# A graph layer and expert kernel on one core: what stands where, and which load comes how, at the changes between its stages

## The chip, the cores and the metric

The kernel runs on one core of a Trainium2 chip. The metric is the device time of one execution in microseconds (us). TensorE (PE in the profile) multiplies, VectorE (DVE) and ScalarE (ACT) work on elements, GpSimd (POOL) and SyncE (SP) mostly start transfers. ACT starts some transfers too; each of these engines works its own instruction list in order.

## The reference: what is computed

```
x = layernorm(x)                                    # 10000 nodes, 512 channels
for l in 0, 1, 2:
    agg = segment_sum(x[src], dst) / max(deg, 1)    # 20000 edges, sorted by dst
    out = agg @ Wl + bl + x @ Wr
    x = where(out >= 0, out, a * out)
x = x0 + x                                          # x0: the input
xn = layernorm(x)
cw = top 2 of softmax(xn @ Wr + br), 8 experts
x = x + sum over e of cw[e] * (relu(xn @ W1[e] + b1[e]) @ W2[e] + b2[e])
```

## The kernel before, in words

Nodes are worked in 79 tiles of 128 rows, edges in 157 tiles of 128. All node rows stay in SBUF in one tensor, `res`. Two buffers serve tiles in turn (slot 0 for even tiles, slot 1 for odd ones), and nearly every semaphore is kept for each slot. Since (agg / deg) @ Wl equals the sum over edges of rows of x @ Wl, each layer has two stages.

**Dense stage** (`dense`, and `first_dense` for layer 0). PE turns a tile of x (`x_transpose`, into psT), ACT and DVE apply the slopes to it in its turned form (`keep_xT` on ACT; `bend` on DVE), and PE makes y = x @ Wl. ACT copies y out (`take_y`), SP stores it to DRAM (`store_y`, y_rows). In layers 1 and 2 a product of full precision is made from three products at a higher rate: `y_high` (w_high, x_high), `y_low` (w_low, x_low) and `y_cross` (w_cross, x_cross). DVE makes x_high, x_low and x_cross for each tile (`high_x`, `split_x`) and, once a layer, the parts of the weights: `split_high` (w_cross and w_part, from the raw weights in wy), `split_cross` (w_high and w_cross) and `split_low` (w_low, which is written over wz, so it waits for the last z product). `next_x` on DVE makes the x of a tile: the gathered sum times 1/deg plus the tile's z.

**Sum stage.** POOL gathers rows of y from DRAM by `src` (`gather_edge`, eight buffers), ACT and DVE split them in two parts (`high`, `low`), PE sums them within an edge tile by a product with a selection matrix (`segment_sum`, L710 and L711), ACT copies the sums out and stores them in DRAM (sum_rows). Between the segment sums PE makes z = x @ Wr (`z_product`, `z_half`), and DVE adds the bias to it and puts it back in `res` (`take_z`). Nine z tiles, the late ones, are kept for the end of the stage. There the sums of segments that run over several edge tiles are mended: PE multiplies the starting rows (L747), DVE adds the result to gathered rows (L1385), POOL scatters them to sum_rows, and only then gathers sums by node (`gather_node`). On DVE the order of all this is written out by hand, between the nine late `take_z`.

**Expert stage.** For each tile two streams are woven together on DVE (`experts`): the part `ahead` makes x, its residual sum with the input rows (loaded by SP into `outs`, `load_x`) and its moments, and ends in POOL's and ACT's `norm`; the part `own` takes the router's logits, finds the top two experts, and adds the bias b1 (in bvec) to the hidden layer. PE's order is in `x_turn`, `router`, `hidden_turn`, `up` and `down`.

Three places where one stage meets the next are touched. wz holds Wr for the z products, but in the dense stage of layers 1 and 2 it holds w_low; so ACT starts Wr's load (`load_z`, L874) only once the last `y_low` is done, and then bl's load, and then copies the last two y tiles out. The raw Wl for the next layer comes from SP near the end of the sum stage. At the end of layer 2 SP loads W1, a, b2, the rows of x for tiles 0 and 1, and then, when all z tiles are taken, b1 (into bvec), W2 (into wz) and the rows of x for tiles 2 and 3.

## Time and profile before

| | us |
|---|---|
| median of 3 runs | 2687.99 |
| lowest and highest | 2687.64, 2690.53 |
| the profiled execution | 2686.95 |
| its span | 2685.2 |
| TensorE busy in it | 2625.3 (98%) |
| VectorE, ScalarE, GpSimd busy | 1805.6, 1272.2, 990.5 |
| mean granted TensorE clock | 0.994 of full speed |

The span runs from the first to the last instruction of the profiled execution; 1.75 us of its time lie outside. TensorE's span holds all stages one after the other, so time is lost where it stands idle or runs at its lower clock. The stages lie about so: dense 0 to 350 us, sums of layer 0 to 676, dense of layer 1 from 702 to 955, its sums to 1315, dense of layer 2 from 1319 to 1575, its sums to 1937, experts to the end.

### The profile page before, as it was taken

What the parts mean: (1) busy time and instruction counts of PE and PEld (TensorE: products, weight loads), DVE (VectorE), ACT (ScalarE), POOL (GpSimd) and SP (SyncE); (2) the same over time, 40 slices, a digit from 0 to 9 for tenths busy, and PEclk for the clock granted to TensorE, in tenths of its full rate; (3) what the DMA queues carried; (4) which work ended last, traced back from release to release, by engine and by line L of the source; (5) the groups of instructions that cost most, each with busy time, mean ns of one, the idle gap of its engine ahead of it and who ended that gap; (6) DMA issues with size and microseconds to landing.
All of it is one profiled execution on the core that took longest, in us unless ns stands there. A gap on an engine that the chain in (4) does not pass through costs nothing.

```text
span 2685.2 us, 39728 instructions
## 1 busy us (share of the span) xinstructions
PE 2625.3 (98%) x9195; PEld 1506.2 (56%) x9195; DVE 1805.6 (67%) x5090; ACT 1272.2 (47%) x2681; POOL 990.5 (37%) x1054
## 2 busy tenths in 40 slices
PE   7999999999999999999999999999899999999999
PEld 3444445554688855555588855555455555555554
DVE  5555555554899955555699955555477777777775
ACT  2222245554588855555388855555122222222222
POOL 2222255553344445554233335555122222222221
PEclk9999999999999999999999999999999999999999
DMA  4444378887355568887355558888422222222221
GB/s 133 133 133 133 118 224 270 266 271 229 100 164 164 164 214 263 274 263 257 97 164 165 164 181 273 263 274 263 145 78 82 82 86 90 82 82 85 87 85 48
DMA packets 200943, 446.57 MB, mean 166 GB/s; under 512 B 34383, under 2 KB 34695, under 8 KB 200836
## 3 DMA queue, kind: packets, MB, share of 16 engines
q0 software_dynamic: 64928, 207.55, 27.2%
q10 hardware_dynamic: 69168, 126.12, 12.9%
q1 hardware_dynamic: 66740, 111.54, 11.9%
q8 instruction: 59, 0.97, 0.1%
q14 instruction: 48, 0.39, 0.0%
HBM read 238.50 MB, written 207.11 MB: 166 GB/s over the span
## 4 chain that ended last, share of the span: by engine, by line
PE 94%; DMA 2%; DVE 2%; ACT 1%; issue 1%; SPq 0%; POOL 0%; DVEq 0%; POOLq 0%; ACTq 0%
PE psY L590 11%; PE psH L570 10%; PE psY L570 10%; PE psM L698 9%; PE psY L698 9%; PE psH L698 8%; PE psT L564 6%; PE psY L604 5%; PE psY L612 5%; PE psY L621 5%; PE psS L710 4%; PE psS L711 4%; PE psM L570 2%; PE psH L590 1%; PE psS L564 1%; PE psH L799 1%
## 5 line engine op out<-in xcount | busy, mean ns | idle before, releaser
L498 POOL DMA_INDIRECT rows<-y_rows,lists x471 | 485.4, 1031 | 475.7 <-PE psS L711 355.0
L1175 DVE TENSOR_TENSOR lows<-rows,highs 128x512 fp32r<-128x512 f32 x471 | 326.2, 693 | 374.1 <-ACT highs L832 366.6
L505 POOL DMA_INDIRECT rows<-sum_rows,nodeI x237 | 296.0, 1249 | 329.7 <-DVE rows L1183 295.7
L832 ACT ACTIVATE outs<-psS 128x512 f32<-128x512 f32 x471 | 279.8, 594 | 284.5 <-PE psS L711 284.0
L832 ACT ACTIVATE highs<-rows 128x512 fp32r<-128x512 f32 x471 | 294.8, 626 | 143.5 <-ACT outs L832 109.7
L710 PE MATMUL psS<-highs,sel 128*128 128x512 f32 x471 | 348.7, 740 | 7.2 <-ACT outs L832 7.2
L479 POOL TENSOR_TENSOR st<-st,small 128x1 f32<-128x1 f32 x158 | 89.9, 569 | 664.1 <-DVE st L1075 664.1
L590 PE MATMUL psY<-wy,res 128*128 128x512 f32 x632 | 286.6, 596 | 0.7 <-ACT res L832 0.7
L570 PE MATMUL psY<-wy,xTs 128*128 128x512 f32 x632 | 285.2, 594 | 0.0
L570 PE MATMUL psH<-wz,hTs 128*128 128x512 f32 x632 | 284.2, 592 | 0.7 <-ACT hTs L832 0.7
L698 PE MATMUL psM<-wz,res 128*128 128x512 f32 x544 | 255.5, 592 | 0.0
L698 PE MATMUL psY<-wz,res 128*128 128x512 f32 x536 | 251.7, 592 | 0.0
L698 PE MATMUL psH<-wz,res 128*128 128x512 f32 x528 | 248.0, 592 | 0.0
L832 ACT ACTIVATE outs<-psY 128x512 f32<-128x512 f32 x237 | 141.8, 598 | 221.3 <-PE psY L590 213.8
L946 ACT ACTIVATE rows<-res,st 128x512 f32 (+1 forms) x79 | 64.2, 813 | 361.4 <-POOL st L547 361.4
L564 PE MATMUL psT<-ident,rows 128*128 128x128 f32 x1264 | 197.5, 279 | 23.0 <-ACT rows L946 8.0
L570 PEld LDWEIGHTS psH<-wz,hTs 128*128 128x128 f32 x632 | 120.0, 190 | 151.7 <-issue 150.7
L843 ACT ACTIVATE res<-psS,acol 128x128 f32 (+1 forms) x632 | 180.7, 369 | 20.8
L604 PE MATMUL psY<-w_high,x_high 128*128 128x512 f32 x632 | 186.6, 417 | 0.0
L711 PE MATMUL psS<-lows,sel 128*128 128x512 f32 x471 | 186.2, 395 | 0.0
L564 PEld LDWEIGHTS psT<-ident,rows 128*128 128x128 f32 x1264 | 145.6, 141 | 67.3 <-issue 45.5
L590 PEld LDWEIGHTS psY<-wy,res 128*128 128x128 f32 x632 | 114.7, 192 | 115.6 <-issue 114.5
(166 smaller groups left out, 4109.7 us busy)
## 6 DMA issues: line engine op xcount, KB each, us to landing
sum_rows<-outs ACTq DMA_DIRECT2D x471, 256.0 KB, 3.7
y_rows<-outs SPq DMA_DIRECT2D x237, 256.0 KB, 2.0
rows<-in_x POOLq DMA_DIRECT2D x78, 256.0 KB, 2.9
outs<-in_x SPq DMA_DIRECT2D x78, 256.0 KB, 2.6
out_rows<-res SPq DMA_DIRECT2D x78, 256.0 KB, 2.0
rows<-y_rows,lists POOLq DMA_INDIRECT x471, 4.2
rows<-sum_rows,nodeI POOLq DMA_INDIRECT x237, 3.5
wy<-in_L_gnn_Wl SPq DMA_DIRECT2D x3, 1024.0 KB, 7.3
```

The source lines that it names most:

```text
L498: pool.indirect_dma_start(out=rows[:, t % RING, :], out_offset=None, in_=y_d, in_offset=bass.IndirectOffsetOnAxis(ap=col(srcT, t), axis=0) ...
L505: pool.indirect_dma_start(out=rows[:, s, :], out_offset=None, in_=s_d, in_offset=bass.IndirectOffsetOnAxis(ap=col(nodeI, t), axis=0), boun ...
L564: mm = pe.transpose(dest[:, c * P:(c + 1) * P], tile[:, c * P:(c + 1) * P], ident[:, :])
L570: mm = pe.matmul(dest, xT[:, c, :], w[:, c, :], start=(c == 0), stop=(last and c == C - 1))
L590: mm = pe.matmul(dest, part(t, c), w[:, c, :], start=(c == 0), stop=(c == C - 1))
L604: mm = pe.matmul(psY[s][:, :], x_high[:, q * P:(q + 1) * P], w_high[:, q, :], start=(q == 0), stop=False, skip_group_check=True)
L698: mm = pe.matmul(psZ(l, s), part(t, q), wz[:, q, :], start=(q == 0), stop=(q == C - 1))
L710: pe.matmul(psS[g % 2][:, :], sel[:, g, :], highs[:, g, :], start=True, stop=False)
L711: pe.matmul(psS[g % 2][:, :], sel[:, g, :], lows[:, t % RING, :], start=False, stop=True)\
L832: act.activation(o, i_, ACT.Copy).then_inc(signal, 1)
L843: x_ = act.activation(part(t, q), psS[s][:, q * P:(q + 1) * P], ACT.Copy, scale=acol[:, k - 1, q:q + 1])
L1175: dve.tensor_tensor(lows[:, t % RING, :], rows[:, t % RING, :], highs[:, g, :].bitcast(F32), ALU.subtract)\
```

## The change

Six edits.

1. The late end of the sum stage, on DVE: the second late `take_z` and the mended rows' additions stand ahead of `split_high`, which waits for the raw weights.
2. Also there: the third tile's x (`next_x(0, 2)`) and the second tile's `bend` stand ahead of `split_low`, and not after the last `take_z`, in the first `split_x`.
3. On PE the third tile's turn stands first in `dense`. In layer 1 the first `y_high` writes the PSUM tile that the last z product filled, so it now waits by name for the last `take_z` there.
4. Wr of layers 1 and 2 is loaded in four parts of 128 rows, each with a semaphore, and the first z product waits for each part ahead of the multiplication that reads it.
5. SP loads the rows of x for tiles 2 and 3 ahead of its wait for all z tiles, so ahead of b1 and W2.
6. DVE waits for b1 ahead of the first addition of it, and not ahead of the whole first `experts`.

```diff
@@ SP
                     for c in range(2):
                         load_x(sp, 0, c, outs, var_in, 1, xe_in)
+                    for c in (2, 3):
+                        load_x(sp, 0, c, outs, var_in, 1, xe_in)
                 all_turns(sp, z_sb, l + 1)
...
-            for c in (2, 3):
-                load_x(sp, 0, c, outs, var_in, 1, xe_in)
@@ PE
             def dense(k):
                 pe.wait_ge(high_parts, k)
+                x_transpose(0, 2, k)
+                if k == 1:
+                    pe.wait_ge(z_sb[0], uses(0))
...
-                    if not (isinstance(i, int) and 2 * i + c + 2 >= NT):
+                    if not (first or isinstance(i, int) and 2 * i + c + 2 >= NT):
                         x_transpose(i, c + 2, k)
...
+            def first_z(l):
+                pe.wait_ge(z_sb[0], l * uses(0))
+                for q in range(C):
+                    pe.wait_ge(wz_row[q], 16 * l)
+                    mm = pe.matmul(psZ(l, 0), part(0, q), wz[:, q, :], start=(q == 0), stop=(q == C - 1))
+                mm.then_inc(z_ps[0], 1)
...
-                pe.wait_ge(wz_in, 16 * (l + 1))
-                z_product(0, 0, l)
+                if l == 0:
+                    pe.wait_ge(wz_in, 16)
+                    z_product(0, 0, l)
+                else:
+                    first_z(l)
...
-            pe.wait_ge(wz_in, 16 * (LAYERS + 1))
+            pe.wait_ge(wz_in, 32)
@@ ACT, load_z
-                act.dma_start(wz[:, :, :], Wr[l].rearrange("(c p) n -> p c n", p=P)).then_inc(wz_in, 16)
+                for q in range(C):
+                    act.dma_start(wz[:, q, :], Wr[l][q * P:(q + 1) * P, :]).then_inc(wz_row[q], 16)
@@ DVE, split_x
                 if not (isinstance(i, int) and i + c == 0):
                     high_x(i, c, k)
-                if not (isinstance(i, int) and 2 * i + c + 2 >= NT):
-                    next_x(i, c + 2, k)
-                if not (isinstance(i, int) and 2 * i + c + 1 >= NT):
-                    bend(i, c + 1, k)
+                    if not (isinstance(i, int) and 2 * i + c + 2 >= NT):
+                        next_x(i, c + 2, k)
+                    if not (isinstance(i, int) and 2 * i + c + 1 >= NT):
+                        bend(i, c + 1, k)
@@ DVE, experts
                     dve.wait_ge(hT_ps[s], n)
+                    if isinstance(i, int) and i + c == 0:
+                        dve.wait_ge(bvec_in, 16 * (LAYERS + 1))
                     k_h = step(dve.tensor_tensor(h, psY[s][:, :], bvec[:, :], ALU.add))
@@ DVE, the end of a layer
                 take_z(*late[0], l)
-                if l + 1 < LAYERS:
-                    split_high(l)
                 take_z(*late[1], l)
...
                        .then_inc(mend_add, 1)
+                if l + 1 < LAYERS:
+                    split_high(l)
                 take_z(*late[2], l)
...
                     take_z(*late[-2], l)
+                    next_x(0, 2, l + 1)
+                    bend(0, 1, l + 1)
                     split_low(l)
                     take_z(*late[-1], l)
...
-            dve.wait_ge(bvec_in, 16 * (LAYERS + 1))
             dve.wait_ge(small_in, 32)
```

On DVE, at the end of layer 0's sums, stood before (res<-psY is `take_z`, rows<-rows,psS the mended rows' additions, w_cross<-wy and w_part `split_high`):

```order
L1164 TENSOR_TENSOR res<-psY,bvec 128x512 x3
L1234 TENSOR_SCALAR w_cross<-wy 128x512 x4
L1235 TENSOR_TENSOR w_part<-wy,w_cross 128x512 x4
L1164 TENSOR_TENSOR res<-psY,bvec 128x512
L1385 TENSOR_TENSOR rows<-rows,psS 128x512
L1385 TENSOR_TENSOR rows<-rows,psS 29x512
L1164 TENSOR_TENSOR res<-psY,bvec 128x512
L1238 TENSOR_TENSOR w_high<-wy,w_part 128x512 x4
```

On DVE at the same place stands now:

```order
L1179 TENSOR_TENSOR res<-psY,bvec 128x512 x4
L1400 TENSOR_TENSOR rows<-rows,psS 128x512
L1400 TENSOR_TENSOR rows<-rows,psS 29x512
L1249 TENSOR_SCALAR w_cross<-wy 128x512 x4
L1250 TENSOR_TENSOR w_part<-wy,w_cross 128x512 x4
L1179 TENSOR_TENSOR res<-psY,bvec 128x512
L1253 TENSOR_TENSOR w_high<-wy,w_part 128x512 x4
```

One `take_z` and both additions moved from behind the eight instructions of `split_high` to ahead of them.

A little later on DVE, at the start of the dense stage of layer 1, stood before (rows<-rows,rdeg,res is `next_x`, res<-psT,res `bend`):

```order
L1164 TENSOR_TENSOR res<-psY,bvec 128x512
L1246 TENSOR_SCALAR w_low<-w_part 128x512 x4
L1164 TENSOR_TENSOR res<-psY,bvec 128x512
L1183 SCALAR_TENSOR_TENSOR rows<-rows,rdeg,res 128x512
L1190 SCALAR_TENSOR_TENSOR res<-psT,res 128x512
L1212 TENSOR_TENSOR x_low<-res,x_high 128x512
L1215 SCALAR_TENSOR_TENSOR x_cross<-x_low,res 128x512
```

On DVE there stands now:

```order
L1179 TENSOR_TENSOR res<-psY,bvec 128x512
L1198 SCALAR_TENSOR_TENSOR rows<-rows,rdeg,res 128x512
L1205 SCALAR_TENSOR_TENSOR res<-psT,res 128x512
L1261 TENSOR_SCALAR w_low<-w_part 128x512 x4
L1179 TENSOR_TENSOR res<-psY,bvec 128x512
L1227 TENSOR_TENSOR x_low<-res,x_high 128x512
L1230 SCALAR_TENSOR_TENSOR x_cross<-x_low,res 128x512
```

Between the last `take_z` and x_low no instruction is left; `next_x` and `bend` moved ahead of w_low.

On SP, at the end of layer 2's sums, stood before (wy<-in_L_ffn_W is W1, wz<-in_L_ffn_W is W2, bvec<-in_L_ffn_b is b1):

```order
L413 DMA wy<-in_L_ffn_W 128x4x64 x8
L367 DMA avec<-in_L_gnn_a 128x512
L417 DMA b2s<-b_rows 32x512
L358 DMA outs<-in_x 128x512 x2
L367 DMA bvec<-in_L_ffn_b 128x512
L364 DMA wz<-in_L_ffn_W 128x4x512
L358 DMA outs<-in_x 128x512 x3
```

On SP there stands now:

```order
L414 DMA wy<-in_L_ffn_W 128x4x64 x8
L368 DMA avec<-in_L_gnn_a 128x512
L418 DMA b2s<-b_rows 32x512
L359 DMA outs<-in_x 128x512 x4
L368 DMA bvec<-in_L_ffn_b 128x512
L365 DMA wz<-in_L_ffn_W 128x4x512
L359 DMA outs<-in_x 128x512
```

Two of the loads of x moved from behind W2 to ahead of b1.

## Rows read from the trace of the kernel before

**Rows 1.** Windows: a dense stage, a sum stage; us, busy of each engine, PEclk, DMA, GB/s

```profile
720.00:940.00 220.00, 220.00 (x1102) 181.65 (x1101) 206.45 (x344) 193.30 (x481) 102.06 (x69) 1.00 0.51 165
975.00:1276.00 301.00, 298.59 (x831) 156.07 (x830) 175.39 (x371) 174.87 (x306) 153.00 (x150) 1.00 0.83 266
```

**Rows 2.** Waits of PE, whole span: line, waited for, total us, times, longest

```profile
PE psT L564 <- issue: 6.4, 2, 3.2
```

**Rows 3.** Timeline, end of layer 0's sums: start us, us, what, idle before

```profile
671.55 1.43 DVE L1234 TENSOR_SCALAR w_cross<-wy 128x512 fp32r<-128x512 f32 x4 [6.25 <-DMA wy<-in_L_gnn_Wl]
...
676.15 1.26 DVE L1385 TENSOR_TENSOR rows<-rows,psS 128x512 f32<-128x512 f32 x2
...
683.86 7.13 PE L590 MATMUL psY<-wz,res 128*128 128x512 f32 x16 [0.44 <-DVE res L1164]
...
700.37 0.69 DVE L1164 TENSOR_TENSOR res<-psY,bvec 128x512 f32<-128x512 f32 x1 [0.15 <-DVE w_low L1246]
...
702.36 0.68 DVE L1212 TENSOR_TENSOR x_low<-res,x_high 128x512 fp32r<-128x512 f32 x1
```

**Rows 4.** Timeline: the mending products of layers 0 and 1, an addition in layer 2

```profile
667.84 3.04 PE L747 MATMUL psS<-rows,hTs 128*128 128x512 f32 x6
...
1286.21 3.04 PE L747 MATMUL psS<-rows,hTs 128*128 128x512 f32 x6
...
1909.93 0.68 DVE L1385 TENSOR_TENSOR rows<-rows,psS 29x512 f32<-29x512 f32 x1 [0.28 <-PE psS L747]
```

**Rows 5.** Chain that ended last, layer 1 to 2: start us, us, what

```profile
1288.31 1.44 DVE w_cross L1234 x4
...
1315.49 3.20 issue
...
1325.32 0.91 PE psY L621 x4
```

**Rows 6.** Windows: PE at the start of layer 2's dense stage, and of the experts

```profile
1318.70:1325.32 6.62, 6.62 (x21) 5.43 (x22) 4.86 (x8) 3.51 (x10) 2.72 (x2) 0.55 0.15 40
701.94:706.00 4.06, 3.66 (x19) 2.85 (x20) 4.03 (x7) 2.75 (x7) 1.74 (x2) 1.00 0.23 65
1950.90:1958.90 8.00, 7.99 (x26) 5.47 (x27) 4.60 (x23) 1.63 (x5) 0.83 (x3) 0.67 0.13 33
```

**Rows 7.** Timeline, from layer 1's dense stage into its sums

```profile
953.20 0.44 ACTq L874 DMA_DIRECT2D wz<-in_L_gnn_Wr  x1
...
959.06 5.40 PE L590 MATMUL psH<-wz,res 128*128 128x512 f32 x8 [3.98 <-DMA wz<-in_L_gnn_Wr]
963.12 1.01 POOL L498 DMA_INDIRECT rows<-y_rows,lists  x1 [22.79 <-DMA y_rows<-outs]
...
966.74 0.63 ACT L832 ACTIVATE highs<-rows 128x512 fp32r<-128x512 f32 x1 [11.03 <-DMA rows<-y_rows,lists]
```

**Rows 8.** Chain that ended last: first z half in layers 1 and 2

```profile
972.25 1.72 PE psM L698 x4
...
1592.84 1.72 PE psM L698 x4
```

**Rows 9.** Transfers by line: KB each, us from issue to landing

```profile
outs<-in_x SPq DMA_DIRECT2D x78, 256.0 KB, 2.6
```

**Rows 10.** Timeline, layer 2: the first z product, POOL's first gather

```profile
1578.65 6.39 PE L590 MATMUL psH<-wz,res 128*128 128x512 f32 x8 [3.97 <-DMA wz<-in_L_gnn_Wr]
1581.31 1.01 POOL L498 DMA_INDIRECT rows<-y_rows,lists  x1 [21.84 <-DMA y_rows<-outs]
```

**Rows 11.** Timeline, start of the experts: PE, DVE, DVE, PE

```profile
1937.88 1.03 PE L570 MATMUL psM<-wgs,xTs 128*128 128x8 f32 x8 [0.78 <-ACT xTs L832]
...
1941.74 0.17 DVE L1266 SCALAR_TENSOR_TENSOR sm<-psM,bgs 128x8 f32<-128x8 f32 x1 [4.34 <-DMA bvec<-in_L_ffn_b]
...
1945.30 0.69 DVE L1280 SCALAR_TENSOR_TENSOR outs<-rows,outs 128x512 f32<-128x512 f32 x1 [2.01 <-DMA outs<-in_x]
...
1950.91 1.09 PE L564 MATMUL psT<-ident,rows 128*128 128x128 f32 x4 [8.03 <-ACT rows L946]
```

More of the change, by code:

```diff
@@ L212, in build @@
         wz_in = sem("wz_in")
+        wz_row = sems("wz_row", C)
         bvec_in = sem("bvec_in")
```

## The prediction

> **What bounds the kernel now.** I read windows first. TensorE (PE) is busy for the whole of a dense stage's 220 us, and for 298.59 of 301 us of a sum stage, at full clock [rows 1]. So inside a stage PE sets the time, and time can only be won where one stage meets the next. The list of PE's waits, the timeline around each meeting, and the chain that ended last then give five places:
>
> - Layer 0 to 1, and 1 to 2: PE waits 3.2 us ahead of the third tile's turn, twice [rows 2]; "issue" there only means that no single record released it. The timeline does: DVE makes w_low, takes the last z, makes the third x, bends, and only then makes x_low, all after the last z product. Ahead of this DVE waits 6.25 us for the raw weights [rows 3], with mended rows and z tiles queued behind that wait.
> - Dense stage to sums, layers 1 and 2: PE waits 3.98 and 3.97 us for Wr, and its next product takes 5.40 and 6.39 us [rows 7, 10], where two products in a row take 7.13 [rows 3], so 3.5 each.
> - Sums to experts: PE waits 8.03 us for the normed third tile [rows 11]. Its work is late because DVE waits 4.34 us for b1, then 2.01 us for the input rows of that tile [rows 11], which were issued behind b1 and W2.
>
> The clock comes on top. After 3.2 us of waiting in layer 2's start the granted clock is 0.55 over 6.62 us, but 1.00 after the same wait in layer 1's, and 0.67 over 8.00 us in the experts' start [rows 6]. The two levels are 1.2 and 2.4 GHz, so 0.55 is nearly all at the lower one.
>
> **Edit 1, mended rows ahead of raw weights.** It takes 1.26 us of additions and one take_z (0.69) from between w_part and the product that waits for DVE, 1.95 us in all [rows 3]. In exchange split_high can start only after the additions: the mending product's start plus its 3.04 us plus an addition of 0.68 [rows 4]. Layer 0: 667.84 + 3.72 = 671.56, against 671.55 when the weights let w_cross start [rows 3]. Nothing is lost, and PE wins **1.9**: product three no longer waits and the later wait is met with DVE 1.9 us further. Layer 1: 1286.21 + 3.72 = 1289.93 against 1288.31 [rows 4, 5], 1.6 later, so **0.3** remains. The mended rows' scatter and the gathers by node start earlier too, but they are behind other work already. Bounds: 0 to 1.9 and -0.5 to 0.3.
>
> **Edits 2 and 3, the third tile.** In layer 1 the z tile's take ends at 700.37 + 0.69 = 701.06, and x_low starts at 702.36 [rows 3]. next_x and bend now stand in the time in which DVE waits for the last z product, so x_low follows the take at once: **1.3**. y_high waits for the same take by name (its PSUM tile), so PE idles as long at first, but it is no later for x_low than DVE.
> In layer 2 the tile is another one, and turn and y_high run at once behind the last z product, T = 1315.49. Before, the first y_cross stands at 1325.32, T + 9.83 [rows 5]. Now DVE is free for x_low at T + 2.3: in layer 1 the wait ended at 701.94 [rows 6] and was 3.2 long [rows 2], so T was 698.74 and the take's end T + 2.3. Four whole-tile instructions of about 0.65 (0.69 by itself, some of it overlapped) give the fourth tile's x at T + 4.9. The five pieces from 1318.70 to 1325.32 are 6.62 x 0.55 = 3.6 us of work at full clock [rows 6]; the last two, a turn (half a product) and a product, are 1.4 of it. So y_cross stands at T + 6.3: **3.5** won, of which 3.0 is the clock. PE's wait is now cut in two, about 1.6 and 1.0 us, and I take it that the clock stays up. If it falls, 1.4 is left. That is the range of the term.
>
> **Edit 4, Wr in quarters.** A 256 KB load of this kind lands in 2.6 us [rows 9]; the whole of Wr took 5.86 (953.20 to 959.06, rows 7). So the first part should land at 955.8 and the last near 959.1, as the bytes are the same. Each multiplication is 0.9 (7.13 / 8, rows 3), so the first z product ends at 960.0 where it ended at 964.46. Two more products end near 967.0. Now something else is late: the first edge. POOL gathers it at 963.12, ACT starts on it at 966.74 for 0.63 [rows 7], DVE needs another 0.69, which is 968.1. The second edge is a gather behind (1.01 and a bit), with half a microsecond of sums: the first z half starts at 969.8 where it was 972.25 [rows 8]: 2.4. Three more issues of 0.44 [rows 7] stand on ACT ahead of its last two copies of y, whose stores POOL's gathers wait for: 0 to 1.3 later. I take 0.8, for part of it is hidden by stores that queue behind the load anyway: **1.7** in layer 1. In layer 2, 1581.31 [rows 10] + 3.62 + 0.63 + 0.69 = 1586.25, with 1.7 again 1587.95, against 1592.84 [rows 8]: 4.9, less 0.8, **4.1**; PE is ready at 1578.65 + 0.94 + 7.0 = 1586.6. Bounds: -1.3 to 2.4 (the clock falls in the new wait of about 2 us; a fall costs up to 6.39 - 3.5 = 2.9, rows 10), and 0.9 to 4.9.
>
> Against this edit speaks the Trainium skill, "DMA: Bandwidth & Descriptors", Rules for kernel authors: for full bandwidth a transfer should have at least 1 MiB. Its Anatomy section fits a transfer, one issued from GpSimd, as about 2.0 us plus its bytes at 436 GB/s. By that fit, an estimate from the page, a quarter is 2.6 us, as the row shows, and four of them are 10.4 us if the fixed parts don't overlap; the sum would then lose nearly all of this edit. The row decides only for one quarter; how four in a queue overlap no row of this load shows.
>
> **Edits 5 and 6, start of the experts.** The logits are there at 1937.88 + 1.03 = 1938.9, and DVE now starts then, not at 1941.74: 2.84. The 2.01 us for the rows of x go too, for they are issued before b1 [rows 11]. PE's turn comes 4.85 earlier, at 1946.06; b1 landed at 1941.7 and its first use is past that. The wait that is left is 8.03 - 4.85 = 3.2 us, as long as the two after which the clock once fell and once didn't. The 8.00 us of work behind it are 8.00 x 0.67 = 5.4 at full clock [rows 6]. So 4.9 are won if the clock falls as before, 7.5 if not; I take the middle, **6.1**. The two loads cost SP nothing: both moments they wait for come before the last z tile.
>
> **Sum.** 1.9 + 1.3 + 0.3 + 3.5 + 1.7 + 4.1 + 6.1 = 18.9. The profiled execution took 2686.95, so 2668.05; the median is 1.04 above it: **2669**. All upper ends give 1.9 + 1.3 + 0.3 + 3.5 + 2.4 + 4.9 + 7.5 = 21.8, or 2666; all lower ends 0 + 1.3 - 0.5 + 1.4 - 1.3 + 0.9 + 4.9 = 6.7, or 2681.
>
> **Rivals.**
> - *Quarters don't overlap.* Each part takes the 2.6 us of a lone one [rows 9], 10.4 in all, so the first z product ends at 953.20 + 10.4 + 0.9 = 964.5, as before: nothing in layer 1, and 0.9 in layer 2, where that product took 1.0 longer. 18.9 - 5.8 + 0.9 = 14.0, 2674. For it: stores and bl's load share the engines. Against it: many transfers are in flight in every stage at 165 to 266 GB/s [rows 1].
> - *The sum stage gives the start back.* Were the gathers and not PE its bound (266 GB/s, a DMA share of 0.83, rows 1), the 5.8 of edit 4 would be gone at its end: 13.1, 2675. Against it: PE's 2.4 us idle in 301.
> - *The clock falls in the new waits* in layer 1's sums, at layer 2's dense start and in the experts: 18.9 - 3.0 - 2.1 - 1.2 = 12.6, 2675.
> - *Slower: the last y stores.* ACT's four issues hold back the copies on which all gathers wait. With a delay of d in both layers edit 4 gives 7.3 - 2 d, and the other edits 13.1, so it decides from d = 10.2 on; 5.4 slower, 2693, is d = 12.9. Against it: ACT's added issues are 1.3 us.
> - *The change does little.* Something not in the records, such as a later release of PE in the experts' start, keeps edits 5 and 6 from counting, and two of the above come with it: under 5 won, 2684.
>
> **Chances.** The forecast 0.70, by itself from 2665 to 2673; quarters 0.08; given back 0.07; clock 0.08; slower 0.02; little 0.05. A difference under 0.2% (5.4 us) can't be told from none here. Faster 0.93, same 0.05, slower 0.02. The range of 2664 to 2676 takes in the first three rivals and leaves out the last two and odd mixtures.
>
> **What would show it.** In the profile after: L1400's additions ahead of L1249, with PE's wait near 676 gone and one of under 1 us near 681; the 3.2 us waits of rows 2 gone or cut, and y_cross of layer 2 some 6.3 us behind the last z product at a granted clock of 1.00; PE's first z product starting less than 1 us after the dense stage, its four parts about 0.9 apart, and the new wait for an edge behind it; POOL's first gather at most 1.3 us later against the load's issue; in the experts no wait for b1 or x and a PE wait of about 3.2 us. The prediction is wrong if the quarters land together at the end, if POOL's first gather moves by more than 2 us, or if the experts' start keeps its 8 us.

## The result, and the profile after

| | before | after |
|---|---|---|
| median of 4 runs, us | 2689.23 | 2671.27 |
| lowest and highest | 2687.64, 2690.53 | 2669.96, 2673.41 |
| ratio of times, 95% interval | | 0.9934 [0.9917, 0.9951] |
| the profiled execution | 2686.95 | 2673.41 |
| its span, its granted clock | 2685.2, 0.994 | 2671.8, 0.997 |

The table of before ahead of the prediction had three of these four runs. The change saves 18.0 us by the medians. The two profiled executions differ by 13.5 only: that of before was faster than all four runs of its median, that of after is the slowest of its four. Of all executions behind this document one was disturbed (before_fill, 10552.56 us at a granted clock of 0.557), and it is left out. The four runs after took 2673.41, 2672.07, 2670.47 and 2669.96 us at a mean granted clock of 0.997, 0.997, 0.998 and 0.999. So the clock is part of the result, and a trace shows one draw of it.

Windows of the changed kernel: the same two steady stretches as in [rows 1], then PE behind its wait at the start of layer 1's dense stage, of layer 2's, and of the experts. The columns are those of [rows 1], PEclk third from the end.

```profile
720.00:940.00 220.00, 220.00 (x1100) 181.68 (x1099) 206.51 (x345) 193.50 (x483) 102.61 (x69) 1.00 0.51 164
975.00:1276.00 301.00, 298.54 (x829) 155.54 (x828) 173.90 (x367) 173.21 (x303) 151.83 (x148) 1.00 0.83 266
701.00:705.93 4.93, 4.93 (x18) 3.85 (x17) 3.99 (x8) 2.31 (x6) 1.32 (x1) 0.65 0.16 37
1314.60:1320.00 5.40, 4.95 (x17) 3.84 (x18) 4.26 (x8) 2.30 (x6) 1.31 (x1) 0.68 0.15 49
1936.70:1945.50 8.80, 8.79 (x26) 5.71 (x27) 4.60 (x23) 2.40 (x6) 1.56 (x4) 0.61 0.11 31
```

The steady stages are as they were. At the three meetings the granted clock behind the waits is 0.65, 0.68 and 0.61, and the waits are shorter now but not gone. The rows of PE's waits that the change touched (line, waited for, total, times, longest):

```profile
PE psT L565 <- ACT rows L961: 2.7, 1, 2.7
PE psH L701 <- DMA wz<-in_L_gnn_Wr: 2.3, 3, 1.0
PE psS L721 <- DVE lows L1190: 2.0, 3, 1.2
PE psY L605 <- DVE res L1179: 1.9, 1, 1.9
PE psY L613 <- DVE x_low L1227: 1.8, 1, 1.8
```

The 3.2 us waits of [rows 2] became 1.9 and 1.8, the waits of 3.98 and 3.97 us for Wr [rows 7, 10] became pieces of at most 1.0, the 8.03 of the experts [rows 11] became 2.7; the wait for an edge's `lows` is new.

Timeline from layer 1's dense stage into its sums (start us, us, what, idle before), against [rows 7]:

```profile
951.78 1.83 ACTq L889 DMA_DIRECT2D wz<-in_L_gnn_Wr  x4
954.68 1.96 PE L701 MATMUL psH<-wz,res 128*128 128x512 f32 x4 [1.02 <-DMA wz<-in_L_gnn_Wr]
954.97 0.89 SPq L373 DMA_DIRECT2D y_rows<-outs  x2
957.00 1.98 PE L701 MATMUL psH<-wz,res 128*128 128x512 f32 x4 [0.36 <-DMA wz<-in_L_gnn_Wr]
958.82 3.60 PE L591 MATMUL psM<-wz,res 128*128 128x512 f32 x8
960.67 1.01 POOL L499 DMA_INDIRECT rows<-y_rows,lists  x1 [21.77 <-DMA y_rows<-outs]
...
967.11 0.47 PE L721 MATMUL psS<-highs,sel 128*128 128x512 f32 x1 [0.64 <-DVE lows L1190]
```

PE starts on the first quarter 2.9 us behind the load's issue, where it started 5.86 behind the issue of the whole. All four quarters are used by 958.8, 7.0 behind the issue. What is late next is the second edge, at 967.11.

The late end of layer 0's sums, against [rows 3]:

```profile
667.27 3.04 PE L761 MATMUL psS<-rows,hTs 128*128 128x512 f32 x6
...
669.45 0.69 DVE L1400 TENSOR_TENSOR rows<-rows,psS 128x512 f32<-128x512 f32 x1 [1.29 <-PE psS L761]
...
671.51 0.68 DVE L1400 TENSOR_TENSOR rows<-rows,psS 29x512 f32<-29x512 f32 x1 [1.37 <-DMA rows<-sum_rows,small]
...
672.12 1.41 DVE L1249 TENSOR_SCALAR w_cross<-wy 128x512 fp32r<-128x512 f32 x4
...
682.67 1.55 PE L591 MATMUL psY<-wz,res 128*128 128x512 f32 x3 [1.86 <-DVE res L1179]
```

The second addition waits for its gathered rows, and `split_high` behind it starts at 672.12.

### The profile page after: what moved, and what is told of

Read it like the earlier page. It is cut to its first block, busy times and chain, and to the rows that moved or that the text cites. A ratio compares the mean times of both kernels' runs of the same rounds, so it can differ in the third digit from the quotient of the medians.

```text
span 2671.8 us, 39734 instructions
## 1 busy us (share of the span) xinstructions
PE 2622.9 (98%) x9195; PEld 1503.3 (56%) x9195; DVE 1806.9 (68%) x5090; ACT 1270.1 (48%) x2681; POOL 990.2 (37%) x1054
## 4 chain that ended last, share of the span: by engine, by line
PE 94%; DVE 2%; DMA 2%; ACT 1%; issue 1%; SPq 0%; ACTq 0%; POOL 0%; another core or an unknown queue 0%; DVEq 0%; POOLq 0%
PE psY L591 11%; PE psH L571 10%; PE psY L571 10%; PE psM L709 9%; PE psY L709 8%; PE psH L709 8%; PE psT L565 6%; PE psY L605 5%; PE psY L613 5%; PE psY L622 5%; PE psS L721 4%; PE psS L722 4%; PE psM L571 2%; PE psS L565 1%; PE psH L813 1%
## 5 line engine op out<-in xcount | busy, mean ns | idle before, releaser
L571 PEld LDWEIGHTS psY<-wy,xTs 128*128 128x128 f32 x632 | 114.6, 191 | 115.4 <-issue 114.4
```

What stands on the lines that cost most here:

```text
L571: mm = pe.matmul(dest, xT[:, c, :], w[:, c, :], start=(c == 0), stop=(last and c == C - 1))
```

## The experiments

All ratios are to the kernel before, run on the same chip in the same batch. Its median was 2687.77 us in the first batch (four kernels, each with part of the change), 2685.73 in the second (four), 2686.53 in the third (four). Beside the times I use steps: how much shorter the way from one place to the next is in a kernel's trace than in before's. At the start of layer 1's and layer 2's dense stage it is the way from the last z product to the first `y_cross`, in the sum stages from Wr's issue to the first z half, in the experts from the second tile's turn to the first `down`.

**Edits 5 and 6 alone.**

```diff
-                    for c in range(2):
+                    for c in range(4):
                         load_x(sp, 0, c, outs, var_in, 1, xe_in)
...
-            dve.wait_ge(bvec_in, 16 * (LAYERS + 1))
...
                     dve.wait_ge(hT_ps[s], n)
+                    if isinstance(i, int) and i + c == 0:
+                        dve.wait_ge(bvec_in, 16 * (LAYERS + 1))
```

> The kernel before with edits 5 and 6 alone (x of tiles 2 and 3 loaded ahead of b1, b1's wait ahead of its first use). Theory (the gain is DVE's chain moved by 4.9 us, and PE's following work stays at the lower clock as before): 4.9 us faster, the PE wait of 8.03 us falls to about 3, and the granted clock over the 8 us behind it stays near 0.6. Rival (the shorter wait keeps the clock up): 7.5 us faster with a granted clock near 1.

Measured 2680.77 us, 0.9978 [0.9969, 0.9987]: 7.0 us by the medians, 5.9 by the ratio. PE's wait at the start of the experts is 2.7, and the clock behind it fell in the profiled execution, as the theory had it:

```profile
1943.40:1951.90 8.50, 8.44 (x26) 5.62 (x27) 4.60 (x23) 1.96 (x6) 1.32 (x3) 0.62 0.11 34
```

The step is 4.72 us.

**Edit 4 alone** (Wr in quarters and `first_z`).

> The kernel before with edit 4 alone (Wr in four loads). Theory (parts land about 0.9 us apart and PE works on each; POOL's gathers start about 1 us earlier too): first z half 3 us earlier in layer 1 and 4.5 in layer 2, some of it given back within the sum stages (0.5 and up to 2), so 5 to 7 us in all. Rival (fixed parts of the four loads don't overlap): under 1 us.

Measured 2683.30 us, 0.9984 [0.9975, 0.9993]. The first z half comes 1.65 us earlier in layer 1 and 4.45 in layer 2; 0.60 and 0.87 of it are gone at the late end of the two sum stages. In all it is a little less than the 5 to 7 us expected, and far from the rival's 1.

**Edit 1 alone** (both additions ahead of `split_high`).

> The kernel before with edit 1 alone (second late z tile and the mended rows' additions ahead of the raw weights). Theory (the second gathered block of starting rows lands late beside the load of the raw weights, so the additions end only 0.5 us or more behind the weights' arrival): 0.6 us in layer 0 and 0.3 in layer 1, about 0.9 in all. Rival (as the prediction had it, the additions are done when the weights land): 1.9 and 0.3, 2.2 in all.

Measured 2686.23 us, 0.9995 [0.9986, 1.0004]: no difference by the interval, so the time doesn't choose between theory and rival. The trace does. The second addition waits for its gathered rows:

```profile
673.07 0.67 DVE L1383 TENSOR_TENSOR rows<-rows,psS 29x512 f32<-29x512 f32 x1 [1.38 <-DMA rows<-sum_rows,small]
```

From the mending product to the product that waits for DVE it is 15.40 us in layer 0, where it was 16.02: 0.62 won, and 0.13 in layer 1, as the theory had it.

**Edits 2 and 3 alone.**

> The kernel before with edits 2 and 3 alone (third tile's x and second bend ahead of the low weights, third turn first on PE). Theory (the order gives 1.3 us in layer 1 and 3.5 in layer 2 at full clock, and a fall of the clock in the split waits takes about 1.2 of each): 2.4 us when the clock falls in both, 4.8 when in neither. Rival (PE is bound by DVE there anyway and the layer 2 turn brings nothing): 1.3 in each, 2.6, with the clock at 1.

Measured 2683.29 us, 0.9991 [0.9982, 1.0000]. The waits are the 1.9 and 1.8 of the changed kernel. The clock fell in both: `y_cross` stands 7.24 and 7.40 us behind the last z product. The interval holds both 2.4 and 2.6, and reaches 4.8.

Beside the prediction's terms the four parts stand so:

| | forecast | gain by the medians | by the ratio, interval |
|---|---|---|---|
| edit 1 | 2.2 | 1.5 | 1.3 [-1.1, 3.8] |
| edits 2, 3 | 4.8 | 4.5 | 2.4 [0.0, 4.8] |
| edit 4 | 5.8 | 4.5 | 4.3 [1.9, 6.7] |
| edits 5, 6 | 6.1 | 7.0 | 5.9 [3.5, 8.3] |
| sum | 18.9 | 17.5 | 13.9 |
| all six at once | 18.9 | 18.0 | 17.7 [13.2, 22.3] |
| all six, again | 18.9 | 13.4 | 15.9 [12.1, 19.6] |

(The last column is one less the ratio, times 2688.) The parts add up within the intervals. Medians are themselves uncertain by some us here: the same kernel gave 18.0 in one batch and 13.4 in the next.

**The changed kernel again**, in the second batch.

> The changed kernel once more, beside its variants on one chip. Theory (the four parts of the change add up, as they lie at different stage changes): 17 to 18 us faster than the kernel before. Rival (parts take from each other): 14 or less.

Measured 2672.31 us, 0.9941 [0.9927, 0.9955]. Its five runs lie at 2675.15, 2672.86, 2667.83, 2672.31 and 2669.66 us with a granted clock of 0.996, 0.996, 0.999, 0.997 and 0.998: the lower the clock, the longer. 17 to 18 us were expected, 14 or less by the rival. The medians' 13.4 falls to the rival, the ratio's 15.9 lies between the two, and its interval holds both, so this run doesn't choose. The three kernels below that differ from the changed one in one detail (mend_split, bl_last, halves) have ratios of 0.9939 to 0.9942, so about 16 us is the better estimate of what the change saves, and 18.0 was on the high side.

**Products in the waits.** PE gets products whose result is overwritten or never read, where it would wait: five ahead of the wait in layer 1's dense start, five in layer 2's, two in the experts'.

```diff
+                if k == 1: fill(psH, 5)
                 if k == 1:
                     pe.wait_ge(z_sb[0], uses(0))
...
                     if first:
+                        if k > 1: fill(psY[1], 5)
                         pe.wait_ge(low_parts, k)
...
             pe.wait_ge(b2_back, 16)
+            for k in range(2):
+                pe.matmul(psS[1][:, :], ident[:, :], wy[:, 0, :], start=True, stop=True)
```

> The changed kernel with added products whose results nobody reads, in PE's waits: five of 128x512 in layer 1's dense start, five in layer 2's, and two of full precision ahead of the third turn in the experts. Theory (the clock falls in these waits and PE's work behind them runs at the lower level): the granted clock behind them stays at 1.00, and the kernel is up to 1.2 us faster in layer 1, 1.2 in layer 2 and 2.6 in the experts than the changed one, 2 to 5 us in all. Rival (the fall has its cause elsewhere, or the added products delay PE as much): no difference, or up to 1 us slower.

Measured 2667.57 us, 0.9928 [0.9914, 0.9942], 4.7 under the median of the changed kernel in the batch. Windows of it, at the experts' start and at the two dense starts:

```profile
1930.00:1939.50 9.50, 7.75 (x34) 4.52 (x33) 6.72 (x31) 3.03 (x7) 1.84 (x3) 1.00 0.30 103
700.00:706.00 6.00, 4.90 (x23) 3.61 (x22) 5.74 (x11) 3.17 (x10) 1.32 (x1) 1.00 0.02 8
1312.00:1320.00 8.00, 6.82 (x34) 5.08 (x32) 7.75 (x15) 4.63 (x12) 1.32 (x1) 1.00 0.19 51
```

The two intervals overlap, but the mean granted clock of its five runs is 0.999 or 1.000. Behind the waits it is 1.00 at all three places, where it was 0.61 in the experts and 0.65 and 0.68 in the dense starts. The step up to the first `down` is 7.01 us (4.52 in the changed kernel). In the experts the fill stood behind the wait for W2, so that wait showed, and the third tile's turn came 0.87 us later than in the changed kernel:

```profile
PE psS L832 <- DMA wz<-in_L_ffn_W: 1.8, 1, 1.8
```

**One addition on each side of split_high.**

```diff
-                for b, r in BLOCKS:
+                for b, r in BLOCKS[:1]:
                     (wait and addition)
                 split_high(l)
+                for b, r in BLOCKS[1:]:
+                    (wait and addition)
```

> The changed kernel with the second block's addition (29 rows) put back behind the split of the raw weights, the first block's left ahead of it. Theory (the gather of the second block is what held DVE in layer 0's end): split_high starts as soon as the weights land, and layer 0's end is about 0.5 us earlier than in the changed kernel. Rival (the raw weights land late themselves): no difference.

Measured 2670.86 us, 0.9939 [0.9926, 0.9953], 1.5 under the changed kernel, too little for the intervals. The timeline of the same stretch as above shows it directly:

```profile
666.45 3.04 PE L761 MATMUL psS<-rows,hTs 128*128 128x512 f32 x6
...
669.61 1.43 DVE L1249 TENSOR_SCALAR w_cross<-wy 128x512 fp32r<-128x512 f32 x4 [0.29 <-DMA wy<-in_L_gnn_Wl]
...
680.72 0.70 PE L591 MATMUL psY<-wz,res 128*128 128x512 f32 x1 [0.73 <-DVE res L1179]
```

From the mending product to the one that waits for DVE it is 14.27 us here, 15.40 in the changed kernel, and 683.86 - 667.84 = 16.02 before [rows 3, 4]. In the kernel called best further down, which has the same order, it is 14.81: there the weights landed 3.69 us behind the mending product, here 3.16.

**bl's load behind the last two copies of y.**

```diff
 (load_z)
-                all_turns(act, xd_set, l)
-                act.dma_start(bvec[:, :], bl[l].partition_broadcast(P)).then_inc(bvec_in, 16)
 ...
                     take_y(PAIRS, 0, l)
+                    all_turns(act, xd_set, l)
+                    act.dma_start(bvec[:, :], bl[l].partition_broadcast(P)).then_inc(bvec_in, 16)
```

> The changed kernel with the load of bl issued behind ACT's last copy of y, not ahead of both last copies. Theory (what POOL's first gather waits for is the last store of y, and ACT's issues stand ahead of its copy): gathers and the first z half start about 0.5 us earlier in layers 1 and 2, so about 1 us faster than the changed kernel. Rival (the store's landing is set by the load of Wr before it in the engines): no difference, or slower where bl lands too late for the first z tile.

Measured 2670.11 us, 0.9941 [0.9928, 0.9955]: the ratio of the changed kernel. Timeline, layer 1:

```profile
949.75 1.83 ACTq L889 DMA_DIRECT2D wz<-in_L_gnn_Wr  x4
...
952.46 0.89 SPq L373 DMA_DIRECT2D y_rows<-outs  x2
...
960.07 1.01 POOL L499 DMA_INDIRECT rows<-y_rows,lists  x1 [23.19 <-DMA y_rows<-outs]
```

The last stores are issued 2.71 us behind Wr's issue and not 3.19, but the gather starts 10.32 behind it, where it was 8.89 and, in the repeat, 10.03. In layer 2 it starts 9.05 behind, where it was 8.50 and 8.49. The theory is refuted: issuing the stores earlier doesn't bring the gathers forward.

**Wr in two halves** (four loads become two of 512 KB, each half waited for once).

> The changed kernel with Wr in two loads of 512 KB instead of four. Theory (behind the first z product the first edge is what PE waits for, so a later first z product costs nothing in layer 1 as long as it ends by then): first z halves in both layers within 0.5 us of the changed kernel's, same time. Rival (the z products lead, so the first part's landing counts): the first part lands 1 us later and about 1 us is lost in each layer.

Measured 2672.04 us, 0.9942 [0.9929, 0.9955], as with quarters. In layer 1 the first z product starts later:

```profile
951.37 0.96 ACTq L890 DMA_DIRECT2D wz<-in_L_gnn_Wr  x2
...
955.47 4.94 PE L702 MATMUL psH<-wz,res 128*128 128x512 f32 x7 [2.21 <-DMA wz<-in_L_gnn_Wr]
```

It starts on the first half 4.10 us behind the issue, and in this execution the clock fell in that wait (0.67 over the 5.13 us from 955.47), so two things made it late. The steps to the first z half are 1.80 and 4.71 (3.02 and 4.51 in the changed kernel's first trace, 1.99 and 4.44 in its second). In layer 2 halves and quarters are the same since the edge is what is late.

**Eight products in before's wait of 8 us**, right behind the second tile's turn.

> The kernel before with eight added products of full precision (6.9 us at full clock), read by nobody, in PE's wait of 8 us at the start of the experts. Theory (the lower clock behind that wait costs 2.6 us by itself): the granted clock behind it is 1.00 and the kernel 2 to 2.6 us faster. Rival (the clock there has another cause): no change.

Measured 2684.24 us (eleven executions), 0.9989 [0.9980, 0.9998], with a granted clock of 1.00 from 1951.10 to 1956.40. Timeline of PE:

```profile
1942.76 7.03 PE L809 MATMUL psS<-wy,ident 128*128 128x512 f32 x16
1951.13 0.63 PE L564 MATMUL psT<-ident,rows 128*128 128x128 f32 x4 [1.34 <-ACT rows L948]
...
1952.99 3.60 PE L570 MATMUL psY<-wy,xTs 128*128 128x512 f32 x8
```

The third tile is no earlier than before (1951.13 against 1950.91, rows 11), but its turn takes 0.63 and not 1.09, and the product behind it 3.60. The step up to the first `down` is 2.35 us. Useless work in a wait wins 2.3 us by the medians and 3.0 [0.5, 5.4] by the ratio, so the lower clock by itself costs two to three us there. The traces agree: from the third turn to the first `down` it is 5.29 us here, and 7.83 to 9.42 in the five traces that have before's work there and no fill.

**Edit 5 alone.**

> The kernel before with edit 5 alone: x of tiles 2 and 3 loaded ahead of b1 and W2, DVE still waiting for b1 ahead of the whole first experts. Theory (DVE's two waits, 4.3 us for b1 and 2.0 for x, follow each other in the one chain): 2.0 us of PE's 8.03 us wait go, and the kernel is 2 us faster. Rival (both waits lie on one another, so only both edits together help): no change.

Measured 2686.09 us, 0.9992 [0.9983, 1.0001]: no difference by the interval.

```profile
1940.71 0.17 DVE L1264 SCALAR_TENSOR_TENSOR sm<-psM,bgs 128x8 f32<-128x8 f32 x1 [4.99 <-DMA bvec<-in_L_ffn_b]
...
1947.79 1.09 PE L562 MATMUL psT<-ident,rows 128*128 128x128 f32 x4 [6.58 <-ACT rows L944]
```

PE's wait is 6.58, not 8.03: the wait for x is gone, but DVE waits 4.99 for b1 and not 4.34, so part of it came back. Edit 6 is needed for the rest. The 1.5 us that the trace shows are too few for the times to show.

**All that helped, together**: the fills (that of the experts ahead of the wait for W2), one addition on each side of `split_high`, and bl's load last.

> The changed kernel with the second block's addition behind the split of the raw weights, bl's load behind the last copy of y, and the added products in PE's waits, those of the experts now ahead of PE's wait for W2 (they are products of which nobody reads the result). Theory (clock and mending wait are separate costs): the fills' 4 to 5 us, 1 us of the mending wait and 0.5 to 1 of bl's load add up, 2665 to 2667, so 20 to 22 us faster than the kernel before. Rival (the gains of the fills and of the rest overlap): no better than the kernel with the fills alone.

Measured 2666.18 us, 0.9920 [0.9907, 0.9932]: 20.3 us faster than before, and 5.9 faster than halves, which stands for the changed kernel in this batch. The kernel with the fills alone, in another batch, was 18.2 faster than its before, and the two intervals overlap. So nearly all of the gain over the changed kernel can be owed to the fills; what the additions and bl add, the times don't tell.

## Why the prediction was right, and where not

2669 was forecast and 2671.27 measured, inside 2665 to 2673. The order of waits changed as forecast, with one exception (the second addition). What the terms were worth is another question, for before's one trace, from which they were taken, had its own luck with the clock. The traces kept give a better base: this table has the mean of each way over the traces that have before's order at the place, less the mean over those that have the changed order (four to seven traces on each side, without those that have a fill or another order just there).

| | forecast | by the traces' means |
|---|---|---|
| edit 1 | 2.2 | 0.9 |
| edits 2, 3 | 4.8 | 3.2 |
| edit 4 | 5.8 | 4.7 (5.9 won, 1.3 given back in the sum stages) |
| edits 5, 6 | 6.1 | 6.1 |
| sum | 18.9 | 14.9 |

The total was forecast 3 to 5 us too high, as the 13.9 by the parts' ratios and the 15.9 of the repeat say too. That 2671.27 comes so near to 2669 is in part luck.

**Edit 1, layer 0, forecast 1.9: the step is wrong.** The prediction put the start of `split_high` at the first addition's end and took both additions as ready. The mending product was indeed done, but the second addition needs its gathered rows too. The chain that ended last shows them:

```profile
662.45 9.04 DMA rows<-sum_rows,small
671.49 0.02 issue
671.51 0.06 DVE rows L1400
```

This gather took 9.04 us, beside the 1 MB load of the raw weights. Before, the addition stood behind `split_high`, and the gather's landing was hidden. The step won 0.62 (16.02 less 15.40), in the repeat 0.80. `split_high` started 4.85 us behind the mending product and not 3.72: these 1.1 us are most of what was missing, and the gather accounts for them. The split order won 1.75 in one trace and 1.21 in another. In layer 1, 0.3 was forecast and 0.1 measured: from the mending product to the waiting one it was 1300.62 - 1286.21 = 14.41 us, and is 1296.55 - 1282.27 = 14.28.

**Edits 2 and 3, forecast 1.3 and 3.5: the order is right, the term for layer 2 is too large.** `x_low` follows the take at once in both layers. Timeline of layer 1's start, then of layer 2's:

```profile
699.17 0.69 DVE L1179 TENSOR_TENSOR res<-psY,bvec 128x512 f32<-128x512 f32 x1 [0.15 <-DVE w_low L1261]
699.89 0.69 DVE L1227 TENSOR_TENSOR x_low<-res,x_high 128x512 fp32r<-128x512 f32 x1
...
1314.61 1.20 PE L613 MATMUL psY<-w_low,x_low 128*128 128x512 f32 x4 [1.82 <-DVE x_low L1227]
1316.25 1.11 PE L565 MATMUL psT<-ident,rows 128*128 128x128 f32 x4 [0.44 <-DVE rows L1198]
1317.01 2.06 PE L605 MATMUL psY<-w_high,x_high 128*128 128x512 f32 x4
1318.87 1.17 PE L622 MATMUL psY<-w_cross,x_cross 128*128 128x512 f32 x4
```

In layer 1 the 1.3 us between the take and `x_low` are now 0.03. But PE waited 1.93 us for the take, and the clock behind it was 0.65: `x_low` to the first `y_cross` takes 4.96 us, where it was 706.28 - 702.36 = 3.92. So the profiled execution gave 1.0 of the 1.3 back against before's, where the clock had stayed up. In layer 2 `y_cross` stands 7.4 us behind the last z product, where 6.3 was forecast at full clock: the two pieces at 2.06 and 1.11 us take nearly twice their time. I had taken it that the clock stays up since the waits got shorter. Over all traces it fell about as often as before, and cost a little less in layer 2. From the last z product's end to the first `y_cross`, in us:

| | clock up | clock fell |
|---|---|---|
| before's order, layer 1 | 7.50 (3 traces) | 8.43 (3) |
| changed order, layer 1 | 6.21 (3) | 7.25 (3) |
| before's order, layer 2 | 7.50 (1) | 8.6 to 9.6 (5) |
| changed order, layer 2 | 6.21 (2) | 7.1 to 7.4 (4) |

With the fills it is 6.2 in both layers. So at the same clock the order wins 1.29 us in either layer, and the step of 3.5 for layer 2, which the two kernels with fills, bl_last and halves do show, is the changed order in a lucky execution against before's in an unlucky one. The forecast read before's 0.55 [rows 6] as a cost that the new order removes; it is a draw that either order can lose. The mean gain there is 2.0 us.

**Edit 4, forecast 1.7 and 4.1: right in its mechanism.** The steps of this pair of traces are 3.02 and 4.51; over all traces the first z half comes 2.6 and 3.3 us earlier, the 5.8 forecast in other shares. The quarters overlap: the trace settles what no row of before showed. The first is usable in 2.9 us and the four are in use by 7.0 us behind the issue. By the fit of the Trainium skill ("DMA: Bandwidth & Descriptors", Anatomy of one DMA — SWDGE (gpsimd) path), an estimate, one quarter takes 2.6 us, and four take 10.4 if their fixed parts add up. The first quarter's 2.9 agrees; the 7.0 of all four doesn't, so the fixed parts of several loads in one queue did not add up here. The term mis-sized is the 0.8 us for three more issues ahead of the copies. From Wr's issue to POOL's first gather it took 8.57 to 10.03 us in layer 1 and 8.18 to 8.60 in layer 2 in the six traces with the single load (9.92 and 8.51 in before's own); the five with four loads and bl ahead of the copies are 0.2 later in the mean, in both layers. Worked out from the timelines, for layer 1:

```
kernel           first gather behind the issue   step to the first z half
only_quarters    10.47                           1.65
bl_last          10.32                           1.67
after_again      10.03                           1.99
fill_both         9.20                           2.87
mend_split        8.90                           3.16
after             8.89                           3.02
best              8.77                           3.39
halves            8.73                           1.80
```

The step follows the gather: the last stores of y land early or late beside the load, by up to 1.7 us from one kernel or execution to the next, and the added issues hardly show in it. (halves is the exception: there PE is late, whose third product ends some 16 us behind the issue.) In layer 2 the gather stands 8.2 to 8.8 behind the issue in six of the eight traces, where it was 8.51 before, and their steps are 4.3 to 4.7. In bl_last and best, the two that issue the stores ahead of bl, it is 9.05 and 9.67, and the steps are 4.0 and 3.2. Of the steps in layer 2 some 1.1 us is before's own bad luck: the kernels that keep the single load show steps of 0.5 to 1.6 there, for its first product took 6.39 us in before's trace at a clock of 0.56.

The rival "the sum stage gives the start back" holds in part. Between the first z half and the mending product the changed kernel loses 0.50 and 2.05 us again, in the repeat 1.79 and 0.72, edit 4 alone 0.60 and 0.87, kernels without edit 4 0.0 to 0.3. With halves, fills and best it is 0.5 to 0.6 in all. Of what was won that is from under a tenth to two fifths, not all of it. Of the 2.05, the timeline shows 1.16 at one place, an edge whose rows ACT split late for no reason that the records give:

```profile
1865.43 0.63 ACT L846 ACTIVATE highs<-rows 128x512 fp32r<-128x512 f32 x1 [2.14 <-issue]
...
1866.95 0.47 PE L721 MATMUL psS<-highs,sel 128*128 128x512 f32 x1 [1.16 <-DVE lows L1190]
```

The kernel with fills lost nothing in that stage, but 0.64 in layer 1's. What makes these waits stays open.

**Edits 5 and 6, forecast 6.1: right.** The waits for b1 and x are gone, and what PE waits for now is POOL's and ACT's norm: 2.70 us where 3.2 was forecast:

```profile
1935.42 0.18 POOL L548 TENSOR_TENSOR st<-st 128x1 f32<-128x1 f32 x1
1935.64 0.81 ACT L961 ACTIVATE rows<-res,st 128x512 f32<-128x512 f32 x1 [1.00 <-POOL st L548]
...
1936.71 1.00 PE L565 MATMUL psT<-ident,rows 128*128 128x128 f32 x4 [2.70 <-ACT rows L961]
```

The step is 4.52 us in this pair of traces, near the 4.9 forecast for a clock that falls, and 0.61 was granted. Medians give 7.0 for these edits alone. Both hold: the profiled execution of before was lucky here. In the three kernels with one part that touch nothing at this place the same step is -1.8, -1.6 and -0.4, and a product that took 4.44 us before takes 6.04 in only_quarters. Against the mean of these four traces, the six with the changed order have won 6.1. With the clock at 1.00 the step is 7.87 in bl_last and 7.86 in best, and 7.01 with the fills that waited for W2; forecast 7.5. The clock stayed up in one of those six traces (bl_last); in the other five it was near 0.6. So the forecast's middle between 4.9 and 7.5 was right, but as an average over the luck of both kernels and not because the clock stays up half the time.

**The clock rival** was given 0.08 at 12.6 us. In the profiled execution the clock fell in both dense starts and in the experts, so two of the rival's three places came true, and one that it had not named. Its largest term, 3.0 us for a fall in layer 1's sums, did not: the first z product kept its time in every trace with quarters, behind waits of about 1 us. That the pair of traces shows 13.5, near its 12.6, is chance. The time of 2671.27 speaks for the forecast, but in one thing the rival was nearer: waits made shorter, to some 2 or 3 us, did not keep the clock up.

**The others.** No store of y came 10 us late, which the slower rival needed, and each part shows a gain in its trace, though edit 1's is too small for the times.

## What to carry to other kernels

Where PE is busy for the whole of every stage, look at the meetings of stages: each wait of 2 to 8 us there is one row of the profile, and what is late next is found by adding up the rows behind it, for each operand of an instruction that is moved and not for one. A large load whose first rows are wanted first can be issued in parts, as far as the next late thing allows. Where a wait can't be removed, products in it kept the clock up here; judge such edits by medians over executions, since a pair of traces differs by one draw of the clock at each wait. For the same reason a low clock in one trace is no sure gain to forecast: look at the same place in several executions first.

## What the runs showed of the hardware

- **The clock behind a short wait is a draw.** Behind waits of 1.8 to 3.2 us the same instructions ran at 1.00 in one execution and 0.55 to 0.68 in another. In the changed order this cost about 1 us in a dense start (6.21 against 7.25) and 3 in the experts (5.29 us from the third turn to the first `down` against 8.30 to 8.65). A place that no edit touches shows the same: PE waits 2.34 us for DVE ahead of the last z product of layer 2, which then takes 3.7 us in seven of the fourteen traces and 5.3 to 5.4 in the other seven. These two rows are from the changed kernel and from only_third:

```profile
1924.09 3.70 PE L591 MATMUL psH<-wz,res 128*128 128x512 f32 x8 [2.34 <-DVE res L1179]
1929.72 5.40 PE L590 MATMUL psH<-wz,res 128*128 128x512 f32 x8 [2.34 <-DVE res L1167]
```

  Behind longer and shorter waits it was no draw here: with the single load of Wr the clock fell behind all twelve waits for it (3.6 to 4.1 us), and with quarters behind none of the waits for one (up to 1.0 us, once 1.6).

  That idle time throttles TensorE to 1.2 GHz is a rule of the Trainium skill ("TensorE: Matmul & The Clock Gate", What's actually happening); this case's granted clocks agree that it happens, and show that it isn't certain behind waits of this length. With products in three such waits it stayed at 1.00, and the time fell by 4.7 us.
- **Four loads of 256 KB in one queue took about as long as one of 1 MB.** Issued some 0.46 us apart, the first was usable 2.9 us behind the issue, and all four were used by 7.0, of which the last multiplication is 0.9, so they had landed by 6.1; the whole was usable 5.86 behind its issue.
- **Small transfers beside a large load were slow.** The last store of y, 256 KB, took 4.37 us in the chain that ended last, where the profile's table of transfers has 2.0 for its kind:

```profile
955.51 4.37 DMA y_rows<-outs
```

```profile
y_rows<-outs SPq DMA_DIRECT2D x237, 256.0 KB, 2.0
```

  The gather of mended rows took 9.04 us beside the load of the raw weights, where the median of its six is 5.4. That the load is the cause is not shown: no run took it away. Issuing the store 0.5 us earlier (bl_last) did not bring the gather that waits for it forward.
